# x's five loads go out on ScalarE's DMA queue instead of SyncE's, in a graph network kernel on one core

## What is computed

```
for _ in range(5):
    s_in  = state @ in_W.T + in_b
    s_out = state @ out_W.T + out_b
    a = concat([A @ s_in, A.T @ s_out, state])
    r = sigmoid(a @ r_W.T + r_b)
    z = sigmoid(a @ z_W.T + z_b)
    h = tanh(concat([A @ s_in, A.T @ s_out, r * state]) @ h_W.T + h_b)
    state = (1 - z) * state + z * h
out = tanh(state @ o1_W.T + o1_b) @ o2_W.T + o2_b
return layernorm(x + out)
```

## Time and profile before

| | |
|---|---|
| median of 3 runs | 980.45 us (980.11 to 981.85) |
| the profiled execution | 983.18 us, span 981.4 us |
| TensorE busy | 961.5 us, 98% of the span |
| VectorE busy | 765.5 us, 78% |
| ScalarE busy | 469.7 us, 48% |
| mean DMA rate over the first seven slices of 24.5 us | 335 to 410 GB/s |

### The profile page before, as it was taken

How to read it: one execution, slowest core, us unless ns; L and a number is a source line. 1 busy time by engine, 2 the same in 40 slices (tenths; PEclk the granted TensorE clock), 3 DMA queues, 4 the chain that set the end, 5 groups by cost and what they waited for, 6 DMA issues and landing times.

```text
span 981.4 us, 12040 instructions
## 1 busy us (share of the span) xinstructions
PE 961.5 (98%) x4507; PEld 443.3 (45%) x4507; DVE 765.5 (78%) x1202; ACT 469.7 (48%) x663; POOL 41.8 (4%) x57
## 2 busy tenths in 40 slices
PE   7999999999999999999999999999999999999996
PEld 3444444444444444444444444444444444455445
DVE  4989989888888688867867876787677787745756
ACT  4657566554345346433634553364335435422444
POOL 0310100000000000000000000000000000031101
PEclk9999999999999999999999999999999999999998
DMA  9999995234730455194025607701571482042101
GB/s 335 364 410 362 378 347 150 59 81 103 209 85 1 120 156 101 38 208 131 0 77 153 146 1 166 189 22 33 155 167 22 102 215 65 16 135 86 44 1 44
DMA packets 199787, 134.36 MB, mean 137 GB/s; under 512 B 62257, under 2 KB 191921, under 8 KB 195761
## 3 DMA queue, kind: packets, MB, share of 16 engines
q1 hardware_dynamic: 197424, 125.20, 44.8%
q0 software_dynamic: 2304, 8.39, 2.2%
HBM read 102.11 MB, written 16.78 MB: 121 GB/s over the span
## 4 chain that ended last, share of the span: by engine, by line
PE 79%; DMA 9%; ACT 5%; DVE 4%; issue 2%; SPq 1%; ACTq 0%; DVEq 0%
PE bank L1960 36%; PE bank L2101 19%; PE bank L2079 11%; PE bank L2093 6%; DMA tmp<-in_adj_t 5%; DMA tmp<-in_adj 4%; PE bank L2109 3%; ACT areg L616 3%; PE bank L2174 1%; PE bank L2196 1%; PE bank L2158 1%; PE bank L1885 1%; SPq L413 0%; ACT pq_words L631 0%; ACT areg L811 0%
## 5 line engine op out<-in xcount | busy, mean ns | idle before, releaser
L1960 PE MATMUL bank<-areg,xop_words 128*128 128x512 fp8e4 x1792 | 389.5, 379 | 0.8 <-DVE pq_words L1496 0.8
L1960 PEld LDWEIGHTS bank<-areg,xop_words 128*128 128x128 f16 x1792 | 174.9, 98 | 213.0 <-DVE pq_words L1496 2.7
L811 ACT ACTIVATE areg<-pq_words 128x512 f16<-128x512 f32 x90 | 56.3, 629 | 163.5 <-DVE pq_words L1496 62.5
L2101 PE MATMUL bank<-areg,pq_words 128*128 128x512 f16 x504 | 122.7, 379 | 0.3 <-DVE pq_words L1607 0.3
L1885 PE MATMUL bank<-areg,xop_words 128*128 128x512 fp8e4 x512 | 112.1, 379 | 4.1 <-ACT areg L616 2.1
L2101 PE MATMUL bank<-areg,w 128*128 128x512 f16 x378 | 90.7, 379 | 0.0
L1532 DVE SCALAR_TENSOR_TENSOR areg<-pq_words,areg 128x512 f16<-128x512 f32 x90 | 62.2, 691 | 32.4 <-ACT areg L811 30.6
L1885 PEld LDWEIGHTS bank<-areg,xop_words 128*128 128x128 f16 x512 | 49.7, 98 | 65.5 <-issue 4.2
L616 ACT ACTIVATE areg<-tmp 128x2048 fp8e4<-128x2048 int32 x31 | 59.2, 1915 | 38.2 <-DMA tmp<-in_adj_t 21.4
L2101 PEld LDWEIGHTS bank<-areg,pq_words 128*128 128x128 f16 x504 | 49.2, 98 | 60.1 <-issue 0.8
L2079 PE MATMUL bank<-pq_words,w 128*128 128x512 f16 x288 | 65.4, 379 | 0.0
(11 more groups left out here) (247 smaller groups left out, 1260.1 us busy)
## 6 DMA issues: line engine op xcount, KB each, us to landing
areg<-kept_operands SPq DMA_DIRECT2D x112, 512.0 KB, 4.3
tmp<-in_adj_t SPq DMA_DIRECT2D x16, 1024.0 KB, 8.2
tmp<-in_adj SPq DMA_DIRECT2D x15, 1024.0 KB, 7.7
kept_operands<-xop_words POOLq DMA_DIRECT2D x11, 512.0 KB, 8.1
kept_operands<-areg SPq DMA_DIRECT2D x4, 1024.0 KB, 10.2
areg<-in_x SPq DMA_DIRECT2D x7, 512.0 KB, 4.8
kept_operands<-tmp POOLq DMA_DIRECT2D x5, 512.0 KB, 3.2
pq_words<-in_gate_w SPq DMA_DIRECT2D x6, 384.0 KB, 5.7
```

The lines of the kernel that those rows point to most:

```text
L811: nc.scalar.activation(y_dst(t, g, name)[:, 0, :], src, ACT.Copy, scale=PSC).then_inc(s_yh, 1)
L1960: last = nc.tensor.matmul(dst[:, :], xop[:, m // 2, operand_block(xo, part, m % 2), :], place8[:, mo, m, :], start=first and m == pairs[0] ...
L2101: last = nc.tensor.matmul(dst[:, :], weights(d, wp), yop[:, d, Y_PLACE[name], xp, :], start=False, stop=final and gate < 2 and d == 1 and ...
```

## The change

The five transfers of x leave SP's program and become the first thing in ACT's. On SP the matrix's first blocks follow the weights and the biases at once. Nothing else differs: the destination, the semaphores and the five parts are the same.

```diff
--- before.py
+++ after.py
@@ block.sync
             sp.dma_start(bias_sb[:, :], bias).then_inc(s_bias, 16)
-            for i, (lo, hi) in enumerate(X_PARTS):
-                sp.dma_start(x_nat[:, lo:hi, :], x_v[:, lo:hi, :]).then_inc(s_x[i], 16)
-
             def load_rows(k):
@@ block.scalar
         def _(act):
+
+            x_parts = x.rearrange("(j p) f -> p j f", p=P)
+            for i, (lo, hi) in enumerate(X_PARTS):
+                nc.scalar.dma_start(x_nat[:, lo:hi, :], x_parts[:, lo:hi, :]).then_inc(s_x[i], 16)
+
             def fold_out(d):
```

## The result

The changed kernel takes **984.22 us** (median of 20 runs, 981.39 to 988.81) where the kernel before takes 980.46 us (20 runs beside it, 979.65 to 982.44): **ratio 1.0037, 95% interval 1.0028 to 1.0045**, slower by 3.8 us. Its profiled execution took 984.61 us with a span of 982.8 us.

What follows compares the result with a forecast made beforehand. TensorE was taken as the bound, busy 961.5 of 981.4 us. First product 6.0 late plus 2.0 of clock, less small absorptions, ended the load stage +7.3, put at 7.1: 980.45 + 7.1 = 987.5 us, range 982.3 to 989.0.

Steps and rivals of the forecast that it cites:

- The turns: DMA engines at the start take one packet from each queue in turn, whatever its size; chance 0.66, all slower.
- x becomes the last of this load: Load start: x lands at 22.9, behind blocks 0 to 2; its last reduce ends at 23.5, not 16.97, +6.6.
- The count of 104 against 128: Packets per engine: SP's 104 through block 2 against x's 128, so x has passed only 104 by then.
- The fold, +0.7: Weight fold at the start: gw 0 comes 0.7 us later beside 16 packets of x, hidden inside the wait for x.
- The first product, +6.0: TensorE's first matrix product starts 6.0 us later than 19.82, near 25.9, released by DVE; bounds 5 and 7.
- The clock, 2.0: After 7 us of idling TensorE restarts at the lower clock: 2.0 us taken, between nothing and 2.6.
- The late stage: Load stage's second half: ACT's cast and blocks from 20 on 7.3 us later, 2.0 us wait shrinks to 1.5, stage ends +7.3.
- The sum: Whole kernel: +7.1, the lower edge of the small losses, on the median 980.45, giving 987.5 us.
- the likeliest case: Turns of one packet, chance 0.66, slower; own range 984.5 to 989.0 us.
- the rival of 4 KB turns: Four packets of x per row of weights: x quick, weights slow, fold ends 4.2 later; 983.7 us, chance 0.14.
- Equal bytes: Queues share by bytes or issue order: gw 0 1.4 us later, x near 16; +0.5 to +1.4, 981.4 us, chance 0.10.
- It changes nothing: First transfers start in the same order and the fold covers the rest: 980.45 us, chance 0.06.

Runs made afterwards that it cites:

- the run with x behind the first weights: Changed kernel, with ACT waiting for the first pair of weights before it issues x: 990.52 us, ratio 1.0095.
- added products: Unread small products before the first matrix product; changed kernel: 56 1.0056, 7 1.0012; kernel before: 4 0.9999; x behind the first weights: 22 1.0086, 15 1.0066.
- hold: Changed kernel, with SP waiting for all of x before it issues block 0 of the matrix: 983.58 us, ratio 1.0030.
- 4 KB rows: Changed kernel, with x's rows dealt to partitions so transfers move rows of 4 KB (2 KB in the last two): 982.85 us, ratio 1.0018.
- the run with the blocks held back: x behind the first weights, plus SP holding block 0 for x's third part and blocks 1 and 2 for all of x: 982.07 us, 1.0004.

## Why the prediction was right, and where its sizes were off

**The turns: right, and shown, where both queues move.** There the two hardware queues take the engines by equal numbers of packets, whatever their size: 1019 to 1013 from 7 to 15 us, 194 to 196 with seven times the bytes, 316 to 316 with rows of 4 KB. The Trainium skill, page DMA: Bandwidth & Descriptors, section Queues, rings and completion order, has each DMA engine go round-robin between queues, a whole packet at a time, and puts a packet at typically 9 to 17 descriptors. The runs agree with the round-robin, but not with turns of so many rows: in the packet records of the run with x behind the first weights, 79% of x's rows begin within 2 ns of the end of another row of x near 20 to 22 us, when x moves alone, and 28% from 14 to 18 us, close to the 22% of chance. In the longer turns of the page most of them would follow another row of x. So what is counted in a turn here is one row, of 1, 3, 4 or 8 KB.

**"x becomes the last of this load", +6.6: the step that was mis-sized.** It measured 20.03 - 17.13 = 2.9 in the first profile (maximum ready) and 1.2 in the second. The count of 104 against 128 took the turns to be kept from the start. They weren't. From 0.8 to 5 us ACT's queue moved twice the packets of SP's:

```profile
q1 hardware_dynamic: 258, 0.47, 37.7%
q10 hardware_dynamic: 536, 0.53, 37.5%
```

From 3 to 4 us it had the engines nearly to itself:

```profile
q10 hardware_dynamic: 343, 0.35, 101.4%
q1 hardware_dynamic: 4, 0.01, 1.6%
```

From 5 to 7 us it still moved 456 packets to 195, so that x had passed nearly half of its 2048 packets when the turns became equal. ACT issues 512 KB at a time from 0.72 us on, and SP issued the first `gw` at 1.20 and the second `iow` at 1.67. Why these waited until about 4 us isn't shown: by turns they should have had every other packet. With the head start taken away the step measured 24.72 - 17.13 = 7.6 where 6.6 was forecast, the first product came 7.2 us later where 6.0 was forecast, the half clock cost 2.8 where 2.0 was, and the median rose by 9.05 us (990.52 - 981.47) where the sum said 7.1. The chain of consequences came as written, with each term somewhat larger.

**The fold, +0.7: too small,** and by the same stretch of x alone. `gw` 0 landed at 5.9 and 6.0 in the two profiles of the changed kernel, 1.2 and 1.3 later, and up to 6.3 in those of its variants with added products. I called it hidden behind x's wait; it was, but with x landing early enough (hold, 4 KB rows) it is the limit.

**The first product, +6.0:** +2.5 and +0.8 in the two profiles, by the two terms above; +7.2 without the head start.

**The clock, 2.0: right in kind.** It fell in one of two profiles of the changed kernel and cost 114.3 - 112.5 = 1.8 us. It costs 2.8 where the idle time is 9.8 us. That it can fall in the kernel before too, near 127 us in its second profile, was not foreseen. It fell after waits of 2.2, 2.4, 3.8 and 9.8 us and stayed up after those of 1.8 us and, in two profiles of the kernel before, of 2.0 and 3.0 us, so the length of the wait alone doesn't decide it in these traces. One reading of the prediction is less firm than it looked: the fold runs at half pace until about 10 us by the earlier trace rows, but the granted clock of that stretch reads 1.00, so that this view doesn't show the half clock there. The estimate of 1.7 us for a restart, worked out in the prediction from the Trainium skill, page TensorE: Matmul & The Clock Gate, section Part 1: The HAM clock gate, is met by the 1.8 us and not by the 2.8.

**The late stage: half right.** ACT's copies ended 3.2 us later and block 20 was issued at 81.96 and not at 78.80, with a DMA gap as I wrote it, but of about 3.5 us (from 79 on) and not 7:

```profile
80.00:82.00 2.00, 2.00 (x11) 0.87 (x9) 1.89 (x9) 2.00 (x4) 0.00 (x0) 1.00 0.00 0
```

But the last cast came only 1.3 us later (126.64 against 125.39): the blocks from 20 on were not "7.3 us later" throughout, they caught up 1.9 of 3.2. TensorE had no late wait in either profile of the changed kernel, so the 2.0 us of the earlier trace rows, of which I let the change take 0.5, went whole. They were no part of a typical execution: the profiled execution of the kernel before lay 2.7 us above its median. Profile against profile the change costs 1.4 us of span, median against median 3.8. I had set a typical change against an untypical profile.

**The sum:** +7.1 forecast, +3.8 measured. The direction and the mechanism held. That the median lies in the range is luck in part: the likeliest case's own range began at 984.5, above the measured 984.22, and the range reached down to 982.3 only to take in the rival of 4 KB turns. That rival is not what happened, for DVE released the first product and the counts are one row each. Equal bytes is out by the same counts. "It changes nothing" holds only where the order is kept, as in the run with the blocks held back, and no run was faster.

What stays open: why ACT's queue had the engines nearly alone at the start, why x's last landing differs by 1.7 us between executions (19.1 and 17.4), and how much of the 3.8 us each of the two delays has in a median run, since only single executions were profiled. Of the clock, the runs say only that half to two thirds of it go with it. No version was found that beats the kernel before.

## What to carry to other kernels

A transfer that was moved to a second queue here didn't become parallel, it took every other packet. Its speed then hung on the row lengths on both sides: 1 KB rows beside 8 KB rows got 0.20 of 1.66 MB. One queue is an order of priority; whoever takes a load out of it should say what may pass it, and hold that back by a wait if it matters. And a profile should be placed among the runs before sums are made on it.

## What was not expected of the hardware

A head start counts: both queues began to issue at 0.72 us, and ACT's moved 536 packets to 258 up to 5 us, with 343 to 4 from 3 to 4 us. Kernels with added products have waits of TensorE for its own instructions far behind them, 1.8 us with 56, 1.2 with 4, 0.5 with 22 and none with 7 or 15. The changed kernel, with none added, has 0.4 in its second profile. No rule in their number is seen here, and the largest is as large as what the clock was worth. Executions of one kernel differ by 4 us and more; between those profiled here without such a wait nearly all of it lies in the load stage, since what is behind the first gate product took 846.0 to 846.2 us.
